# Feature products spread over four steps, x tiles requested before the last query store, prologue and exponentials reordered, x1 reloaded in small parts

## The chip, the cores and the metric

The kernel runs on one core of a Trainium2 chip. TensorE multiplies, VectorE, ScalarE and GpSimd (POOL) do the elementwise work, SyncE issues nearly all DMAs. The metric is device time in microseconds of one execution. The engines run their own instruction streams in order and meet at semaphores.

## The reference

Two layers over N = 4096 rows of D = 512, with a symmetric sparse matrix adj (4096 x 4096):

```python
q, k, v = x @ Wq.T + bq, x @ Wk.T + bk, x @ Wv.T + bv
a = q @ k.T / sqrt(512) + adj + adj
x = layernorm(x + softmax(a) @ v)              # layer 0
feats = einsum('nf,hfd->hnd', x, W)            # layer 1, 8 heads of 64
dense = leaky_relu(e_self + e_neigh) + NEG_INF * (1 - adj)
out = relu(softmax(dense) @ feats + b)
x = layernorm(x + out)
```

With NEG_INF = -1e10 and values of adj up to 5.4, each row of layer 1 picks the neighbour with the largest adj (the kernel proves this on the way, and has a general path that isn't run here). So layer 1 is: compute feats for all rows, find each row's largest entry of adj, gather that row of feats, add, normalise.

## The kernel before

All products are made of two float16 parts (high and low): a product of two such operands is three matmuls. Q and K are folded: scores are (x M + c) x^T with M = Wq^T Wk.

**Prologue.** Eight groups g of 512 rows. TensorE computes for each group four value tiles (48 matmuls, banks S0 and S1 in turn, `split_product` on line 635; the third tile waits until VectorE has emptied the bank, `vf_set`) and then the query product (48 matmuls into O0 to O3). ScalarE makes high parts (`x_hi`, `value_hi`, `query_hi`), VectorE empties the value banks (`value_rows`, L979) and makes low parts (`x_lo`, `value_lo`: L963, `query_lo`: L996). GpSimd adds values crosswise (`value_sums`). Per pair of value tiles the chain is GpSimd, ScalarE, VectorE, and GpSimd's buffer is single. SyncE stores x (`x_scratch`), value sums (`vsum_scratch`) and queries (`y_scratch`) and then loads adj and x tiles for the main loop.

**Main loop.** 16 blocks b of 256 query rows, 16 chunks k of 256 keys; c = 16 b + k. One pass of the loop, a step s, has on TensorE the scores of chunk s (24 matmuls, L607) and the values of chunk e = s - 19 (21 matmuls, L684). Per step come 2 x tiles of 256 KB (`xring`, a ring of NX = 5), adj^T (256 KB), value sums (128 KB, a ring of 3), and about one piece of adj (256 KB) for the search of the largest entry. For chunk e: VectorE adds adj (`add`, L1101), takes maxima (L1113), later subtracts the maximum (`subtract`, L1094), ScalarE takes the exponential (L901), GpSimd sums halves (L556, L557), VectorE differences (L1079), ScalarE copies the high parts (L808, narrow 128x128 and wide 128x768), GpSimd makes the low parts (L567, L570), and TensorE multiplies. In the last block VectorE makes the wide low part instead (`last_lo`, L1087). Buffers `pfc` and `pc` are double.

When block b is through its values, its "turn" comes at step 16(b+1)+19: VectorE combines the banks (`combine`), normalises two row tiles j = 0, 1 (`statistics`, `normalise_x1`, at offsets 1 and 2, and 3 and 4 from the turn), and TensorE transposes x1 (8 matmuls, L724) at offset 3 + 2j and multiplies it by W1 (`feats`, 12 matmuls of 512 columns, L735) at offset 4 + 2j, all into bank X. The four W1 tiles of a row tile (`xring<-w_scratch`, 256 KB each) go through the same ring as x. VectorE empties X (`evict_feats`, L1179), and the next tile's transposes wait for that (`f_set`). `block_at(s, offset)` gives the block that stands at that offset; SyncE waits in the same order (`x1_set`, `f_set`) to store x1 and feats. The order of loads is the list `stream`.

**End.** x1 is reloaded in four parts of 2 MB (the last 1.5 MB) during the last block (`load_x1`). After the last block's feats are stored, GpSimd issues 32 indirect loads of feats rows (L589), VectorE and ScalarE add and normalise eight groups, and SyncE stores them.

## Time and profile before

| | us |
|---|---|
| median of 3 runs | 1775.04 |
| lowest, highest | 1771.71, 2446.5 |
| profiled execution, its own time | 1778.22 |
| its span, first to last instruction | 1776.3 |
| TensorE busy | 1600.0 (90%) |
| VectorE busy | 1352.9 (76%) |
| GpSimd busy | 1245.2 (70%) |
| ScalarE busy | 621.6 (35%) |

The chain of work that ended last is 64% TensorE, 11% VectorE, 8% GpSimd, 7% DMA. In the views, PE is TensorE's matmuls, PEld its weight loads, DVE VectorE, ACT ScalarE, POOL GpSimd, SPq SyncE's queue; L607 is line 607 of the kernel; "out<-in" names the tiles; a bracket gives the idle time ahead of an instruction and what ended it. A matmul row's length overlaps the next by about 0.16 us, so steps are read from start to start. The clock column is the share of 2.4 GHz that TensorE was granted.

### The profile page before, as it was taken

The page shows a single profiled execution, that of the slowest core. Times are in us where ns is not written, and L with a number is a line of the kernel's source. Part 1 is how long each engine was busy: PE and PEld are TensorE (multiplying, and loading weights), DVE is VectorE, ACT ScalarE, POOL GpSimd, SP SyncE. Part 2 cuts the span into 40 slices and gives each one's busy share as a digit, 9 for nine tenths or more (in the row PEclk, how much of TensorE's full clock was granted, in tenths as well). Part 3 has the DMA queues.
Part 4 walks back from the last instruction along what each step waited for, and adds up shares of the span by engine and source line. Part 5 has one row for each costly group of instructions (what it writes and reads, how often), then busy time and mean ns, then how long its engine had stood idle before and what let it go on. Part 6 is the DMA issues. An engine that isn't in the chain of part 4 may idle for free.

```text
span 1776.3 us, 36165 instructions
## 1 busy us (share of the span) xinstructions
PE 1600.0 (90%) x13172; PEld 1283.5 (72%) x13172; DVE 1352.9 (76%) x2241; ACT 621.6 (35%) x1085; POOL 1245.2 (70%) x1461
## 2 busy tenths in 40 slices
PE   7798979999999999999999999999999999997820
PEld 3333468888888888888887878788888787875600
DVE  5544437887988888888797888788888888877646
ACT  4343402333333333333332333333333333333427
POOL 3323304988887888788887888888888888886533
PEclk9899989999999999999999999999999999998955
DMA  6434278888888888888888888888888888881668
GB/s 240 151 112 146 107 243 290 265 263 271 260 282 259 287 255 294 263 290 255 280 257 265 262 282 262 276 260 282 263 291 259 284 258 276 252 266 57 200 209 292
DMA packets 281859, 438.13 MB, mean 247 GB/s; under 512 B 26960, under 2 KB 127312, under 8 KB 281680
## 3 DMA queue, kind: packets, MB, share of 16 engines
q1 hardware_dynamic: 276560, 419.01, 73.3%
q0 software_dynamic: 5120, 16.78, 2.9%
q8 instruction: 106, 1.74, 0.4%
q14 instruction: 73, 0.60, 0.1%
HBM read 390.60 MB, written 45.09 MB: 245 GB/s over the span
## 4 chain that ended last, share of the span: by engine, by line
PE 64%; DVE 11%; POOL 8%; DMA 7%; issue 5%; ACT 4%; SPq 1%; ACTq 0%; DVEq 0%; POOLq 0%
PE S L607 32%; PE O L684 26%; DMA xring<-w_scratch 5%; PE X L735 3%; DVE big L963 2%; POOL big L589 1%; POOL pfc L556 1%; POOL pc L570 1%; DMA vsum<-vsum_scratch 1%; PE X L724 1%; DVE pfc L1079 1%; POOL pfc L557 1%; POOL pfc L525 1%; DVE cand L1052 1%; DVE big L1101 1%
## 5 line engine op out<-in xcount | busy, mean ns | idle before, releaser
L607 PE MATMUL S<-yb,xring 128*128 128x256 f16 x6144 | 710.2, 273 | 11.4 <-DMA xring<-x_scratch 11.4
L607 PEld LDWEIGHTS S<-yb,xring 128*128 128x128 f16 x6144 | 602.5, 98 | 84.9 <-issue 11.9
L684 PE MATMUL O<-big,pc 128*128 128x256 f16 (+1 forms) x4608 | 599.8, 276 | 11.8 <-DMA vsum<-vsum_scratch 5.8
L808 ACT ACTIVATE pc<-pfc 128x128 f16<-128x128 f32 (+1 forms) x512 | 289.1, 574 | 862.1 <-PE O L684 549.0
L684 PEld LDWEIGHTS O<-big,pc 128*128 128x128 f16 x4608 | 453.2, 99 | 80.8 <-issue 7.8
L570 POOL TENSOR_TENSOR pc<-pfc,pc 128x768 f16<-128x768 f32 x240 | 396.0, 1650 | 137.1 <-ACT pc L808 136.1
L1101 DVE TENSOR_TENSOR big<-S,big 128x512 f32<-128x512 f32 x256 | 175.6, 686 | 177.5 <-PE S L607 177.0
L556 POOL TENSOR_TENSOR pfc<-pfc 128x256 f32<-128x256 f32 x256 | 233.1, 911 | 79.8 <-ACT pfc L901 79.1
L1113 DVE TENSOR_TENSOR mx<-mx,big 128x512 f32<-128x512 f32 x240 | 238.6, 994 | 8.2
L565 POOL TENSOR_TENSOR sacc<-sacc,pfc 128x256 f32<-128x256 f32 x240 | 212.6, 886 | 0.0
L1079 DVE TENSOR_TENSOR pfc<-pfc 128x256 f32<-128x256 f32 x256 | 186.4, 728 | 0.1
L901 ACT ACTIVATE pfc<-big 128x512 f32<-128x512 f32 x256 | 157.2, 614 | 60.2 <-DVE big L1094 60.1
L1094 DVE TENSOR_TENSOR big<-BC,big 128x512 f32<-128x512 f32 x256 | 173.8, 679 | 2.2 <-PE BC L713 1.4
L1052 DVE MAX8 cand<-piece 128x8 f32<-128x512 f32 x256 | 172.4, 679 | 1.8 <-DMA piece<-in_adj 1.8
L567 POOL TENSOR_TENSOR pc<-pfc,pc 128x128 f16<-128x128 f32 x256 | 116.2, 454 | 79.3 <-ACT pc L808 78.9
L557 POOL TENSOR_TENSOR pfc<-pfc 128x128 f32<-128x128 f32 x256 | 152.5, 596 | 0.0
L684 PE MATMUL O<-vsum,pc 128*128 128x256 f16 x768 | 127.4, 275 | 0.0
L523 POOL TENSOR_TENSOR pfc<-big 128x512 f32<-128x512 f32 x16 | 20.2, 1266 | 151.5 <-DVE big L979 104.9
L735 PE MATMUL X<-xring,x1T 128*128 128x512 f16 x384 | 96.5, 394 | 23.0 <-DMA xring<-w_scratch 20.4
L735 PEld LDWEIGHTS X<-xring,x1T 128*128 128x128 f16 x384 | 36.2, 100 | 71.0 <-DMA xring<-w_scratch 33.4
L684 PEld LDWEIGHTS O<-vsum,pc 128*128 128x128 f16 x768 | 75.8, 99 | 9.3
L607 PE MATMUL S<-big,xring 128*128 128x512 f16 x192 | 49.5, 421 | 15.4 <-DVE big L979 15.1
(130 smaller groups left out, 1190.8 us busy)
## 6 DMA issues: line engine op xcount, KB each, us to landing
xring<-x_scratch SPq DMA_DIRECT2D x512, 256.0 KB, 3.9
big<-in_adjT SPq DMA_DIRECT2D x256, 256.0 KB, 4.2
piece<-in_adj SPq DMA_DIRECT2D x256, 256.0 KB, 3.9
vsum<-vsum_scratch SPq DMA_DIRECT2D x256, 128.0 KB, 3.3
xring<-w_scratch SPq DMA_DIRECT2D x128, 256.0 KB, 3.9
big<-in_xT SPq DMA_DIRECT2D x8, 1024.0 KB, 8.3
yb<-y_scratch SPq DMA_DIRECT2D x16, 512.0 KB, 4.8
hc<-in_x SPq DMA_DIRECT2D x32, 256.0 KB, 4.7
```

The costliest lines, as they stand in the source:

```text
L556: pool.tensor_tensor(buf[:, 512:768], buf[:, 0:256], buf[:, 256:512], ALU.add).then_inc(sums_set, 1)
L565: pool.tensor_tensor(total, total, buf[:, 512:768], ALU.add).then_inc(sum_done, 1)
L570: pool.tensor_tensor(parts[:, 1, P:7 * P], buf[:, 3 * P:9 * P], parts[:, 0, P:7 * P], ALU.subtract).then_inc(lo_rest, 1)
L607: mm = pe.matmul(psum, sta(a, k), mov(b, k), start=(k + a + b == 0), stop=(k == n - 1 and a == 1))
L684: mm = pe.matmul(dst, pc[:, e % 2, a, sta * P:(sta + 1) * P], mov, start=start, stop=(k == NP - 1 and a == 1 and closes))
L735: mm = pe.matmul(X[:, :], x1T[:, a, kc, :], weights[:, m, :], start=(kc + a + m == 0), stop=(kc == KC - 1 and a == 1))
L808: return nc.scalar.activation(dst, src, ACT.Copy, scale=scale)
L1052: dve.max(cand[:, q, :], piece[:, p % NSC, :]).then_inc(cand_set, 1)
L1079: dve.tensor_tensor(buf[:, 768:1024].rearrange("p (k n) -> p k n", k=2), quarters[:, :, 1, :], quarters[:, :, 0, :], ALU.subtract).then_in ...
L1094: dve.tensor_tensor(slot, BC[:, :].rearrange("p (o n) -> p o n", o=1).broadcast_to([P, 2, QB]), slot, ALU.subtract).then_inc(sub_done, 1)
L1101: dve.tensor_tensor(slot, S[c % 2][:, :], slot, ALU.add).then_inc(add_done, 1)
L1113: dve.tensor_tensor(mx[:, :], mx[:, :], slot, ALU.max).then_inc(max_done, 1)
```

## The change

1. A row tile's feature product is spread: its four parts kc go into four successive steps, offsets 4 to 7 for j = 0 and 9 to 12 for j = 1; transposes at offsets 3 and 8, evictions at 7 and 12. The last block keeps all four in one step, at offsets 4 and 6, but uses banks S0 and X for the transposes and O0 and O1 for the products, and evicts at 7 and 8. LAST grows by 6 steps.
2. SyncE issues the first 3 adj and 5 x tiles at the start of the last prologue group. TensorE's wait for all value sums (`v_lo`) moves from the scores to the first values.
3. In the prologue VectorE makes x's low part of the next group behind the first two value rows, and both ScalarE and VectorE handle two query parts ahead of the second value pair.
4. In the main loop ScalarE takes the exponential of chunk e+1 ahead of the copies of chunk e.
5. x1 is reloaded in 15 parts of 512 KB, one a step, from chunk 242 on.

The diff, cut (`load_passing` and `load_adj` moved up unchanged):

```diff
-        LAST = turn(NB - 1) + 8
+        LAST = turn(NB - 1) + 14
...
 
+
+        def transposes_at(s, j):
+            b = block_at(s, 3 + 5 * j)
+            last = block_at(s, 3 + 2 * j)
+            return last if last == NB - 1 else b if b is not None and b < NB - 1 else None
+
+        def feats_at(s, j):
+            parts = [(block_at(s, 4 + 5 * j + kc), kc) for kc in range(KC)]
+            last = block_at(s, 4 + 2 * j)
+            if last == NB - 1:
+                return [(last, kc) for kc in range(KC)]
+            return [(b, kc) for b, kc in parts if b is not None and b < NB - 1]
+
+        def evict_at(s, j):
+            b = block_at(s, 7 + 5 * j)
+            last = block_at(s, 7 + j)
+            return last if last == NB - 1 else b if b is not None and b < NB - 1 else None
+
+        def x1_bank(t):
+            return S[0][:, :] if t == NT - JB else X[:, :]
+
+        def feats_bank(t):
+            return X[:, :] if t < NT - JB else O[t % JB][:, :]
+
+
         def passing():
             for s in range(LAST):
                 for c in scores_at(s):
                     yield s, ("x", c, 0)
                     yield s, ("x", c, 1)
                 for j in range(JB):
-                    b = block_at(s, 4 + 2 * j)
-                    if b is not None:
-                        for kc in range(KC):
-                            yield s, ("w", b * JB + j, kc)
+                    for b, kc in feats_at(s, j):
+                        yield s, ("w", b * JB + j, kc)
 
         stream = list(passing())
...
+                if g == NG - 1:
+
+                    for c in range(AHEAD):
+                        load_adj(c)
+                    for k in range(2):
+                        sp.wait_ge(x_out[k], 16 * (NG // 2))
+                    sp.wait_ge(yp_ready, (NG - 1) * KC)
+                    for i in range(NX):
+                        load_passing(i)
                 if g + 2 < NG:
                     load_x(g + 2)
...
-            def load_x1(e):
-                first, last = 2 * e * EG, min(2 * (e + 1) * EG, NT - JB)
+            def load_x1(b):
+                first, last = b * JB, (b + 1) * JB
                 for j in range(JB):
-                    sp.wait_ge(x1_out[j], 16 * (last // JB))
+                    sp.wait_ge(x1_out[j], 16 * (b + 1))
 
...
                 sp.dma_start(x1r[:, first:last, :],
-                             x1_d[first * P:last * P, :].rearrange("(j p) n -> p j n", p=P)).then_inc(x1r_in[e], 16)
-
-            for c in range(AHEAD):
-                load_adj(c)
-            for k in range(2):
-                sp.wait_ge(x_out[k], 16 * (NG // 2))
-            sp.wait_ge(yp_ready, (NG - 1) * KC)
-            for i in range(NX):
-                load_passing(i)
+                             x1_d[first * P:last * P, :].rearrange("(j p) n -> p j n", p=P)).then_inc(x1r_in[b // 4], 16)
+
...
-                    b = block_at(s, 4 + 2 * j)
+                    b = evict_at(s, j)
...
-                e, r = divmod(s - (NC - NP + 6 + LAG), 5)
-                if r == 0 and 0 <= e < NE // 2:
-                    load_x1(e)
+                if 0 <= s - (NC - NP + 2 + LAG) < NB - 1:
+                    load_x1(s - (NC - NP + 2 + LAG))
...
+                if e == 0:
+                    pe.wait_ge(v_lo, NP)
                 pe.wait_ge(vs_in[e % NVS], (e // NVS + 1) * 16)
...
                 if t % JB == 0:
                     pe.wait_ge(rinv_set, t // JB + 1)
-                else:
+                elif t < NT - JB:
                     pe.wait_ge(f_set, t)
+                dst = x1_bank(t).bitcast(F16)
                 for a in range(2):
                     for kc in range(KC):
-                        mm = pe.transpose(X16[:, (a * KC + kc) * P:(a * KC + kc + 1) * P], x1h[:, a, kc * P:(kc + 1) * P],
+                        mm = pe.transpose(dst[:, (a * KC + kc) * P:(a * KC + kc + 1) * P], x1h[:, a, kc * P:(kc + 1) * P],
                                           ident16[:, :])
                 mm.then_inc(x1T_done, 1)
 
-            def feats(t):
-                pe.wait_ge(x1T_set, t + 1)
-                for kc in range(KC):
-                    i = place["w", t, kc]
-                    weights = xring[:, i % NX, :].rearrange("p (a n) -> p a n", a=2)
-                    pe.wait_ge(x_in[i % NX], (i // NX + 1) * 16)
-                    for a, m in ((0, 0), (0, 1), (1, 0)):
-                        mm = pe.matmul(X[:, :], x1T[:, a, kc, :], weights[:, m, :], start=(kc + a + m == 0),
-                                       stop=(kc == KC - 1 and a == 1))
-                    mm.then_inc(f_part, 1)
+            def feats(t, kc):
+                if kc == 0:
+                    pe.wait_ge(x1T_set, t + 1)
+                    if t >= NT - JB:
+                        pe.wait_ge(c_added, 8 * NB)
+                i = place["w", t, kc]
+                weights = xring[:, i % NX, :].rearrange("p (a n) -> p a n", a=2)
+                pe.wait_ge(x_in[i % NX], (i // NX + 1) * 16)
+                for a, m in ((0, 0), (0, 1), (1, 0)):
+                    mm = pe.matmul(feats_bank(t), x1T[:, a, kc, :], weights[:, m, :], start=(kc + a + m == 0),
+                                   stop=(kc == KC - 1 and a == 1))
+                mm.then_inc(f_part, 1)
 
...
-            pe.wait_ge(v_lo, NP)
             for s in range(LAST):
...
-                    b = block_at(s, 3 + 2 * j)
+                    b = transposes_at(s, j)
                     if b is not None:
                         transpose_x1(b * JB + j)
-                    b = block_at(s, 4 + 2 * j)
-                    if b is not None:
-                        feats(b * JB + j)
+                    for b, kc in feats_at(s, j):
+                        feats(b * JB + j, kc)
...
-                query_hi(g, 0)
+                for jc in range(2):
+                    query_hi(g, jc)
                 value_hi(2 * g + 1)
-                for jc in range(1, KC):
+                for jc in range(2, KC):
                     query_hi(g, jc)
...
@@ -881,6 +908,15 @@
                     scaled(cb[:, 1, 0:DHALF], O[1][:, 0:DHALF], 1.0).then_inc(c_copied, 1)
                     act.wait_ge(o_done, 3 * b + 3)
                     scaled(cb[:, 0, DHALF:D], O[2][:, 0:DHALF], 1.0).then_inc(c_copied, 1)
...
+                e = s - LAG + 2
+                if 0 <= e < NC:
...
+                    nc.scalar.activation(pfc[:, e % 2, 0:512], ring[:, e % SLOTS, :], ACT.Exp, scale=-2.0
+                                         ).then_inc(exp_done, 1)
                 e = s - LAG + 1
                 if 0 <= e < NC:
                     if e >= 2:
...
                     act.wait_ge(sums_set, 2 * e + 2)
                     act.wait_ge(diff_set, e + 1)
                     scaled(pc[:, e % 2, 0, P:7 * P], buf[:, 3 * P:9 * P], 1.0).then_inc(hi_done, 1)
-                e = s - LAG + 2
-                if 0 <= e < NC:
...
-                                         ).then_inc(exp_done, 1)
                 for j in range(JB):
                     b = block_at(s, 2 + 2 * j)
                     if b is not None:
@@ -909,13 +936,14 @@
                             act.wait_ge(x1T_done, t)
                         src = xr[:, j, :] if b < NB - 1 else x1r[:, t, :]
                         scaled(x1h[:, 0, :], src, X1_UP).then_inc(x1_hi, 1)
-                    b = block_at(s, 3 + 2 * j)
+                    b = transposes_at(s, j)
                     if b is not None:
                         t = b * JB + j
                         act.wait_ge(x1T_done, t + 1)
                         if t >= 1:
                             act.wait_ge(f_part, t * KC)
-                        scaled(x1T[:, :, :, :].rearrange("p a c n -> p (a c n)"), X16, 1.0).then_inc(x1T_set, 1)
+                        scaled(x1T[:, :, :, :].rearrange("p a c n -> p (a c n)"), x1_bank(t).bitcast(F16), 1.0
+                               ).then_inc(x1T_set, 1)
...
-                for i in range(GT):
+                for i in range(2):
+                    value_rows(g * GT + i)
+                if 1 <= g < NG - 1:
+                    x_lo(g + 1)
+                for i in range(2, GT):
                     value_rows(g * GT + i)
                 value_lo(2 * g)
-                query_lo(g, 0)
+                for jc in range(2):
+                    query_lo(g, jc)
                 value_lo(2 * g + 1)
-                for jc in range(1, KC):
+                for jc in range(2, KC):
                     query_lo(g, jc)
-                if g + 2 < NG:
-                    x_lo(g + 2)
...
-                dve.scalar_tensor_tensor(out=cb[:, j, :], in0=X[:, :], scalar=1.0 / (W_UP * X1_UP), in1=b1b[:, :],
+                dve.scalar_tensor_tensor(out=cb[:, j, :], in0=feats_bank(t), scalar=1.0 / (W_UP * X1_UP), in1=b1b[:, :],
...
-                    b = block_at(s, 4 + 2 * j)
+                    b = evict_at(s, j)
...
-                    dve.wait_ge(x1r_in[e // 2], 16)
+                    dve.wait_ge(x1r_in[e // 2], 16 * 4 if e < NE - 2 else 16 * 3)
```

What stands in a row on VectorE in the prologue, at the start of group 3 (the groups count from 0). Before (L963 on `hc` or `xring` is x's low part, L979 the value rows, L996 the query parts, L963 on `big` and `vsum` the values' low parts):

```order
L963 SCALAR_TENSOR_TENSOR xring<-big,xring 128x512 x4
L1036 TENSOR_REDUCE u<-big 128x4x8
L979 SCALAR_TENSOR_TENSOR big<-S,big 128x512 x4
L963 SCALAR_TENSOR_TENSOR big<-big 128x512
L963 SCALAR_TENSOR_TENSOR big<-pfc,big 128x1024
L963 SCALAR_TENSOR_TENSOR vsum<-pfc,vsum 128x256
L996 TENSOR_TENSOR yb<-pfc,yb 128x2x256
L963 SCALAR_TENSOR_TENSOR big<-big 128x512
L963 SCALAR_TENSOR_TENSOR big<-pfc,big 128x1024
L963 SCALAR_TENSOR_TENSOR vsum<-pfc,vsum 128x256
L996 TENSOR_TENSOR yb<-pfc,yb 128x2x256 x3
```

After (L991, L1007 and L1024 are the same three):

```order
L1024 TENSOR_TENSOR yb<-pfc,yb 128x2x256 x2
L1067 TENSOR_REDUCE u<-big 128x4x8
L1007 SCALAR_TENSOR_TENSOR big<-S,big 128x512 x2
L991 SCALAR_TENSOR_TENSOR xring<-big,xring 128x512 x4
L1007 SCALAR_TENSOR_TENSOR big<-S,big 128x512 x2
L991 SCALAR_TENSOR_TENSOR big<-big 128x512
L991 SCALAR_TENSOR_TENSOR big<-pfc,big 128x1024
L991 SCALAR_TENSOR_TENSOR vsum<-pfc,vsum 128x256
L1024 TENSOR_TENSOR yb<-pfc,yb 128x2x256 x2
L991 SCALAR_TENSOR_TENSOR big<-big 128x512
L991 SCALAR_TENSOR_TENSOR big<-pfc,big 128x1024
L991 SCALAR_TENSOR_TENSOR vsum<-pfc,vsum 128x256
```

x's low part has moved from the end of the group into the middle of the value rows, and two query parts stand ahead of the second three value parts. The reduce (L1036, then L1067) stays where it was.

On TensorE, the feature product of a block's first row tile. Before (L607 scores, L724 transposes, L735 feature product, L684 values):

```order
L724 MATMUL X<-ident,x1h 128x128 x8
L684 MATMUL O<-big,pc 128x256 x3
L684 MATMUL O<-vsum,pc 128x256 x3
L684 MATMUL O<-big,pc 128x256 x15
L607 MATMUL S<-yb,xring 128x256 x24
L735 MATMUL X<-xring,x1T 128x512 x12
```

After (L750 transposes, L630 scores, L763 feature product, L709 values):

```order
L750 MATMUL X<-ident,x1h 128x128 x8
L709 MATMUL O<-big,pc 128x256 x3
L709 MATMUL O<-vsum,pc 128x256 x3
L709 MATMUL O<-big,pc 128x256 x15
L630 MATMUL S<-yb,xring 128x256 x24
L763 MATMUL X<-xring,x1T 128x512 x3
L709 MATMUL O<-big,pc 128x256 x3
L709 MATMUL O<-vsum,pc 128x256 x3
L709 MATMUL O<-big,pc 128x256 x15
L630 MATMUL S<-yb,xring 128x256 x24
L763 MATMUL X<-xring,x1T 128x512 x3
```

Twelve matmuls in a row have become three in each of four steps, of which two are shown.

On ScalarE, around a block's turn. Before (L808 with `hc` are the combine's copies, with `pc` the high parts, L901 the exponential):

```order
L808 ACTIVATE hc<-O 128x2x256
L808 ACTIVATE hc<-O 128x256 x2
L808 ACTIVATE pc<-pfc 128x128
L808 ACTIVATE pc<-pfc 128x768
L901 ACTIVATE pfc<-big 128x512
L808 ACTIVATE pc<-pfc 128x128
```

After (L918 is the exponential):

```order
L834 ACTIVATE hc<-O 128x2x256
L834 ACTIVATE hc<-O 128x256 x2
L918 ACTIVATE pfc<-big 128x512
L834 ACTIVATE pc<-pfc 128x128
L834 ACTIVATE pc<-pfc 128x768
L918 ACTIVATE pfc<-big 128x512
```

The exponential has moved from behind the two copies to in front of them.

## Rows read from the trace of the kernel before

**Rows 1.** Busy time by stage: window, its length, busy time (instructions), clock, DMA share, GB/s
```profile
42.70:203.80 161.10, 137.12 (x578) 58.81 (x577) 83.74 (x115) 64.22 (x92) 49.73 (x42) 0.89 0.37 128
203.80:224.50 20.70, 20.70 (x97) 9.28 (x95) 9.65 (x15) 8.41 (x15) 6.79 (x6) 1.00 0.30 114
...
370.10:1532.70 1162.60, 1131.23 (x10013) 970.59 (x10012) 976.79 (x1591) 396.64 (x716) 956.36 (x1122) 1.00 0.85 270
```

**Rows 2.** Prologue in time, TensorE: start us, length, instruction [idle before <- releaser]
```profile
110.61 7.86 PE L607 MATMUL S<-big,hc 128*128 128x512 f16 x24 [4.21 <-DVE big L979]
...
138.49 1.89 PE L607 MATMUL S<-big,xring 128*128 128x512 f16 x4 [4.48 <-DVE big L979]
```

**Rows 3.** The same view, VectorE in the same two groups
```profile
105.27 2.50 DVE L963 SCALAR_TENSOR_TENSOR xring<-big,xring 128x512 f16<-128x512 f32 x4 [1.11 <-ACT xring L808]
...
128.66 0.42 DVE L963 SCALAR_TENSOR_TENSOR vsum<-pfc,vsum 128x256 f16<-128x256 f32 x1
```

**Rows 4.** Instructions in time, TensorE, where the scores start
```profile
236.07 4.21 PE L607 MATMUL S<-yb,xring 128*128 128x256 f16 x19 [11.42 <-DMA xring<-x_scratch]
```

**Rows 5.** DMA issues: tile, queue, count, KB each, us to landing
```profile
xring<-w_scratch SPq DMA_DIRECT2D x128, 256.0 KB, 3.9
...
big<-x_scratch SPq DMA_DIRECT2D x3, 2048.0 KB, 8.3
```

**Rows 6.** Instructions in time, TensorE: the row sums that close a block
```profile
370.14 0.50 PE L696 MATMUL X<-vup,sacc 128*128 128x1 f32 x4
...
1532.69 0.51 PE L696 MATMUL X<-vup,sacc 128*128 128x1 f32 x4
```

**Rows 7.** The same view: a wait for weights, and two steps in a row
```profile
948.39 1.33 PE L735 MATMUL X<-xring,x1T 128*128 128x512 f16 x3 [2.16 <-DMA xring<-w_scratch]
...
1241.00 2.78 PE L607 MATMUL S<-yb,xring 128*128 128x256 f16 x24
...
1245.91 2.78 PE L607 MATMUL S<-yb,xring 128*128 128x256 f16 x24
```

**Rows 8.** Who waited for whom, main loop: us in total, times, longest
```profile
PE X L735 <- DMA xring<-w_scratch: 18.7, 17, 2.4
...
PE X L724 <- DVE hc L1179: 10.1, 9, 1.6
...
PEld X L724 <- DVE x1h L963: 4.5, 8, 1.2
```

**Rows 9.** Instructions in time, all engines, at a block's turn
```profile
1182.01 0.41 DVE L1079 TENSOR_TENSOR pfc<-pfc 128x256 f32<-128x256 f32 x1
1182.35 0.68 DVE L1094 TENSOR_TENSOR big<-BC,big 128x512 f32<-128x512 f32 x1
1182.52 0.84 ACT L808 ACTIVATE pc<-pfc 128x768 f16<-128x768 f32 x1 [3.54 <-DVE pfc L1079]
...
1189.08 1.63 POOL L570 TENSOR_TENSOR pc<-pfc,pc 128x768 f16<-128x768 f32 x1
...
1191.23 0.49 PE L684 MATMUL O<-big,pc 128*128 128x256 f16 x3
```

**Rows 10.** Instructions in time, last block: VectorE, ScalarE and TensorE
```profile
1658.21 0.97 DVE L1087 TENSOR_TENSOR pc<-pfc,pc 128x768 f16<-128x768 f32 x1 [0.62 <-ACT pc L808]
...
1661.15 0.61 ACT L901 ACTIVATE pfc<-big 128x512 f32<-128x512 f32 x1
1661.27 0.98 DVE L1087 TENSOR_TENSOR pc<-pfc,pc 128x768 f16<-128x768 f32 x1 [0.62 <-ACT pc L808]
...
1661.85 0.31 ACT L808 ACTIVATE pc<-pfc 128x128 f16<-128x128 f32 x1
...
1666.28 0.82 PE L684 MATMUL O<-big,pc 128*128 128x256 f16 x3 [4.50 <-DMA vsum<-vsum_scratch]
...
1667.53 4.05 PE L684 MATMUL O<-big,pc 128*128 128x256 f16 x18
...
1701.02 0.61 PE L724 MATMUL X<-ident,x1h 128*128 128x128 f16 x8 [0.87 <-DVE hc L1179]
```

56 lines of the change are left out of this document (27 added, 29 removed).

## The prediction

> **What bounds the kernel now.** I read the busy time by stage first, then the order of instructions inside one period of each stage, and the table of waits last. The program has four stages. In the prologue (42.7 to 203.8 us for six of eight groups) TensorE is busy 137 of 161 us at a granted clock of 0.89, and one group without waits takes 20.7 us at full clock [rows 1]. The main loop (370.1 to 1532.7 us) is TensorE's: busy 1131 of 1163 us, clock 1.00, while the DMA engines are 85% busy [rows 1]. Then comes the last query block, in which only values are multiplied, and an end in which indirect loads, VectorE and ScalarE work and TensorE doesn't.
>
> **Prologue.** TensorE waits 4.21 us in the middle of a group's value rows for VectorE, and a group later 4.48 us again; from one such restart to the next it is 27.88 us [rows 2]. The 24 matmuls behind the wait take 7.86 us. What VectorE does while TensorE stands is the low half of x (2.50 us, started only at 105.27) and then a reduce, and only then the value rows that free the PSUM bank [rows 3]. The change puts this x work behind the first two value rows, so that it lies beside the two value tiles that TensorE has by then (20.7/8 = 2.6 us each). It also lets the second query copy go ahead of the second value pair on both engines. The serial chain of value sums (GpSimd, ScalarE, VectorE, twice a group) is not shortened, but in the group that restarts at 110.61 its second round was over at 129.1, 18.5 us later [rows 3], and so fits in 20.7 us. I work the six groups as 6 x 20.7 = 124. Added to that: group 1 keeps a split of W1 behind x's high half, in all about 8 us of ScalarE and VectorE work behind the group's end where TensorE can cover 5.2, hence 3.2 us, perhaps with a slow restart of 1.5 us; groups 2 and 3 keep the reduce, 0.3 us each. Sum 129.5 against 161.1: **31 us gained**, bounds 22 (four of six waits go) and 36 (all, full clock).
>
> *A rule weighed here.* The wait costs more than its length: matmuls ran at half speed for a while, granted clock 0.89 over the stage. The Trainium skill ("TensorE: Matmul & The Clock Gate", Part 1) says that the clock is low by default and that only sustained activity releases it; by that, removing short waits returns more than the waits, which the trace bears out (7.86 us for 24 matmuls that take 20.7/4 = 5.2). The same rule speaks against the change at the end, below.
>
> **Start of the scores.** The prologue's last matmul ends at 224.5 [rows 1], the first scores start at 236.07, after a wait of 11.42 us for x tiles [rows 4], whose requests stand behind the last value and query stores in SyncE's queue. They move ahead of these: five tiles are in the ring long before 224.5, and the scores start at once. But VectorE's last query part is only ready some 3 us after TensorE, and the sixth tile still stands behind that store and three value-sum loads (1.3 us): issued about 4.5 us after the prologue's end, landing 3.9 us later at best [rows 5], 8.5 to 9.5 us. Five tiles last 5 x 1.31 = 6.6 us. So a new stall of 2 to 3 us takes the place of 11.6: **9 us gained**, bounds 6 and 11.
>
> **Main loop, feature matmuls.** From the row sums at 370.14 to those at 1532.69 lie 13 blocks [rows 6], 89.4 us each. A clean step (24 score and 21 value matmuls) is 4.91 us (1241.00 to 1245.91) [rows 7]. 16 steps are 78.6; two feature products of 12 matmuls at 0.216 us 5.2; transposes, broadcast, row sums and the wider first matmuls 2.7: 86.5 us. The other 2.9 us are waits. Before, a tile's four weight tiles follow each other in a ring of five. The fourth is requested only when the step's first x tile is used up, 3.2 us before its turn, and takes 3.9 us or more [rows 5]; so the last three matmuls wait, 2.16 us in the row at 948.39, after which they run slow [rows 7]. In total TensorE waits 18.7 us for weights, and its weight loads longer; and 10.1 us because the next tile's transposes want the bank that VectorE has yet to empty [rows 8]. After the change each step of a feature tile has two x tiles and one weight tile, the step is 5.56 us, and a tile is requested five uses ahead: at least 6.9 us. The second tile's transposes come one step (4 us) after the eviction. Both waits go. DMA per time falls in these steps (1.4 MB in 5.56 us, before 2.2 MB in 7.5), the rate of the others. What stays is the wait for x1's low half (4.5 us of the weight loads' waits over the 13 blocks, 0.3 each [rows 8]). Gain 2.6 us a block, bounds 1.5 and 2.9.
>
> **Main loop, exponentials first.** ScalarE now does the exponential of e+1 ahead of the copies of e. That costs the copies the subtraction (0.68), the exponential (0.61) and handoffs: they come about 1.2 us later, and GpSimd's low part behind them. In plain steps its result has 3 us to spare after that. At a block's turn it has less: the subtraction starts at 1182.35, ScalarE's wide copy at 1182.52, and the next but one low part ends at 1189.08 + 1.63 = 1190.7, TensorE wants it at 1191.23 [rows 9]. A shift of 1.1 us makes it late by 0.5 to 0.6 us, once a block; what this delays further on would otherwise wait for x1. Costs 0.55 a block, bounds 0 (the shift is hidden) and 1.6 (each of three steps late). Net 2.05 us on 14 blocks: **29 us gained**. Where the cover is gone: were the low part late in every step, each tenth of a us would cost 24 us over 240 steps.
>
> **Last block.** Here VectorE makes the low part itself. Before, a step is 3.06 us (1658.21 to 1661.27) [rows 10], since ScalarE's copies and exponential and GpSimd's sums form a ring. With the exponential first, VectorE's low part of e waits for its own subtraction, then the exponential 0.61, the copies 0.31 and 0.84, then 0.97 itself, and a difference of 0.41 and a subtraction of 0.68 follow [rows 9, 10]: with what overlaps and the handoffs 3.6 us. Over the steps 240 to 255, with what TensorE's backlog hides, I count the last start of values 8 to 11 us later by this alone. Against it, the x1 reloads in 2 MB parts (8.3 us to landing) [rows 5] held back the small value-sum loads behind them: a wait of 4.50 us, behind which 18 matmuls take 4.05 us [rows 10], and a shorter one 12 us later. Parts of 512 KB, one a step, end that: 7 to 8 us back. Sum **2.5 us lost**, bounds 12 lost and 6 gained. The low clock belongs to the bound: a step of 3.6 us leaves TensorE idle 1.3, and at the speed shown behind the wait of 4.50 a step's 21 value matmuls take 4.05 x 21/18 = 4.7 us, which is more than the step.
>
> *A rule against this part.* The 2 MB parts landed in 8.3 us, 247 GB/s each alone, a 256 KB tile in 3.9 us, 67 GB/s [rows 5]. The Trainium skill ("DMA: Bandwidth & Descriptors", Rules for kernel authors) wants at least 1 MiB per DMA. By it 15 parts, one after another at the small tile's latency, would be 59 us against 33. By the trace that changes nothing here, for the parts are issued over 15 steps (some 50 us) and nobody wants them before the last block is done.
>
> **After it.** The last tile's transposes use another bank and needn't wait 0.87 us for VectorE [rows 10]; the end is as before. 0.9 us gained.
>
> **Sum.** 1778.2 us is the profiled execution's own time (span 1776.3 and 1.9 around it); less 31, 9, 29 and 0.9, plus 2.5: 1710.8. The median of the runs shown is 1775.0, 3.2 below it; on that scale 1707.6. I say 1708.
>
> **Rivals.**
> - *The turns take it back.* The late low parts cost 1.6 us a block and the feature gain is the low bound of 1.5: the main loop then gives nothing, 1708 + 29 = 1737; half of it 1722. For it: GpSimd is busy 956 of 1163 us [rows 1], so it catches up slowly. Against: its slack in plain steps. Chance 0.17, mostly 1722 to 1737.
> - *The prologue gain stays away*, because the value-sum chain and not the x work sets the group: 1708 + 25 = 1733. For it: the chain runs twice for 9 us. Against: the last group, which has no x work, takes 20.7 us with the same chain [rows 1]. Chance 0.08.
> - *Slower.* ScalarE's new order makes GpSimd the bound in every step: its own work is 4.6 us (956.4 over 208 steps [rows 1]) of the 4.91 to 5.6 of a step, and it breaks even with the whole gain when each of the 240 steps takes 0.29 us longer; at 0.5 us it is 1828. It decides from the point at which the low part ends after 7.5 us of its step's start; I work it to end at 4.4. Chance 0.03.
> - *No reload stall and no cost of the order in the last block*, and all waits gone: 1708 - 13 = 1695 or less. Chance 0.1.
>
> **How the numbers follow.** The forecast (1697 to 1722) has 0.62. From 1690 to 1732 lie the forecast, the better case and most of the first rival, about 0.82. A measurement of this kernel can tell about 2%, that is 1739.5 us. Faster 0.89 (all but the tails of the first two rivals and the third), same 0.08, slower 0.03.
>
> **What would show it.** Right: prologue groups of 20.7 us and its end near 194; scores from there without a gap, with one stall of 2 to 3 us before the sixth tile; blocks of 87.4 us without a wait on weights; a PE wait of about 0.5 us for GpSimd's low part two steps into a block; VectorE's low parts 3.6 us apart in the last block and no wait on value sums. Wrong: groups over 23 us, blocks over 89, feature matmuls that wait for weights, or TensorE at the 1.2 GHz level through the last block.

## The result, and the profile after

The changed kernel takes 1747.1 us (median of 4 runs, 1745.7 to 1751.3). The kernel before took 1774.6 us beside it; the ratio is 0.985, 95% interval 0.983 to 0.988. The gain is 27.5 us where 67 were forecast, and the time lies 25 us above the forecast range (1697 to 1722) and 15 above the wider one (1690 to 1732). The profiled execution took 1745.7 us (span 1743.9; before 1776.3). The spans of the two profiled executions differ by 32.4 us, more than the medians, for the one before was 3.6 us above its median and the changed one 1.4 below; the stages below are compared by these.

The changed kernel by windows: the prologue's six groups, the start of the scores up to the first row sums, the 13 blocks of the main loop, and the last two blocks. Columns: window, length, busy time of PE, PEld, DVE, ACT and POOL with instruction counts, clock, DMA share, GB/s:

```profile
42.70:193.84 151.14, 145.34 (x672) 65.25 (x671) 110.44 (x128) 72.86 (x105) 67.36 (x48) 1.00 0.47 166
193.84:330.34 136.50, 131.99 (x1180) 116.40 (x1179) 104.04 (x145) 29.14 (x55) 73.37 (x87) 0.99 0.85 273
330.34:1495.17 1164.83, 1134.68 (x10012) 967.49 (x10011) 1049.03 (x1591) 384.95 (x715) 954.33 (x1120) 1.00 0.85 270
1495.17:1654.76 159.59, 131.91 (x1084) 106.27 (x1083) 116.62 (x181) 57.32 (x108) 117.82 (x150) 0.95 0.61 192
```

The prologue's end (first row) and the start of the scores came as forecast. TensorE in time, changed kernel, where the prologue ends; three waits are left in the six groups, the longest of them here at 72.03:

```profile
72.03 5.35 PE L630 MATMUL S<-big,xring 128*128 128x512 f16 x24 [3.48 <-DVE big L1007]
...
193.84 6.71 PE L630 MATMUL S<-yb,xring 128*128 128x256 f16 x60
202.69 7.52 PE L630 MATMUL S<-yb,xring 128*128 128x256 f16 x52 [2.13 <-DMA xring<-x_scratch]
```

193.84 answers to 224.50 in [rows 1], and the scores follow without a gap where they started at 236.07 [rows 4]; the new stall of 2.13 us stands before the sixth x tile. The row sums at 370.14 and 1532.69 [rows 6] now stand at:

```profile
330.34 0.50 PE L721 MATMUL X<-vup,sacc 128*128 128x1 f32 x4
...
1495.17 0.51 PE L721 MATMUL X<-vup,sacc 128*128 128x1 f32 x4
```

So 39.8 us had been won at the first mark and 37.5 at the second: 13 blocks take 89.6 us each, before 89.4, forecast 87.4. From 1495.17 to the last row sums at 1654.76 are 159.6 us, before 151.7 (1532.69 to 1684.35): 7.9 us lost. These are the last two blocks: 84.0 and 75.6 us, before 82.8 and 68.9. From there to the end are 89.2 us, before 92.0: 2.8 us won. -39.8 + 2.3 + 7.9 - 2.8 = -32.4, the difference of the spans.

The waits that answer to [rows 8], changed kernel, 330 to 1495 us:

```profile
PEld O L709 <- issue: 40.9, 48, 1.7
...
PE O L709 <- POOL pc L593: 21.8, 34, 1.3
...
PEld X L750 <- DVE x1h L991: 10.7, 13, 2.2
...
PE X L750 <- DVE x1h L991: 7.2, 8, 1.9
...
PEld X L763 <- DMA xring<-w_scratch: 0.5, 2, 0.3
```

The waits for weights (18.7 us) and for the emptied bank (10.1) have gone, as forecast. In their place TensorE waits 21.8 us for GpSimd's wide low part (its weight loads stand still for 40.9 us ahead of the values, in part the same time), and longer for x1's low part (7.2 us against 2.0 before). The 34 waits for GpSimd's low part fall into two kinds. Two steps into each of the 13 blocks there is one of 0.20 to 0.74 us, 0.52 in the mean, in six blocks with a short one of 0.17 or 0.26 in the step behind it. The rest, 13.8 us or 1.06 a block, stand later, among the feature steps, and are 0.38 to 1.26 us long.

### The profile page after: what moved, and what is told of

Read it like the earlier page. It is cut to its first block, busy times and chain, and to the rows that moved or that the text cites. A ratio compares the mean times of both kernels' runs of the same rounds, so it can differ in the third digit from the quotient of the medians.

```text
span 1743.9 us, 36188 instructions
## 1 busy us (share of the span) xinstructions
PE 1590.0 (91%) x13172; PEld 1276.3 (73%) x13172; DVE 1452.9 (83%) x2241; ACT 607.6 (35%) x1085; POOL 1257.9 (72%) x1461
## 3 DMA queue, kind: packets, MB, share of 16 engines
q8 instruction: 106, 1.74, 0.4%
## 4 chain that ended last, share of the span: by engine, by line
PE 54%; DVE 18%; POOL 11%; issue 11%; ACT 5%; DMA 2%; SPq 1%; DVEq 0%; ACTq 0%; POOLq 0%
PE S L630 27%; PE O L709 19%; POOL pc L593 4%; PE O L630 3%; DVE pfc L1110 3%; DVE big L1125 3%; PE X L763 3%; DVE big L1132 2%; ACT pc L834 2%; ACT x1h L834 1%; POOL pfc L579 1%; POOL big L612 1%; DVE cand L1083 1%; DVE mx L1144 1%; DVE big L991 1%
## 5 line engine op out<-in xcount | busy, mean ns | idle before, releaser
L630 PE MATMUL S<-yb,xring 128*128 128x256 f16 x6144 | 709.2, 273 | 2.1 <-DMA xring<-x_scratch 2.1
L630 PEld LDWEIGHTS S<-yb,xring 128*128 128x128 f16 x6144 | 602.1, 98 | 74.8 <-DMA xring<-x_scratch 2.4
L709 PE MATMUL O<-big,pc 128*128 128x256 f16 (+1 forms) x4608 | 600.2, 275 | 42.1 <-POOL pc L593 25.9
L709 PEld LDWEIGHTS O<-big,pc 128*128 128x128 f16 x4608 | 448.3, 99 | 141.6 <-issue 65.9
L918 ACT ACTIVATE pfc<-big 128x512 f32<-128x512 f32 x256 | 161.3, 630 | 949.8 <-DVE big L1125 945.7
L593 POOL TENSOR_TENSOR pc<-pfc,pc 128x768 f16<-128x768 f32 x240 | 407.6, 1698 | 52.8 <-ACT pc L834 52.7
L1144 DVE TENSOR_TENSOR mx<-mx,big 128x512 f32<-128x512 f32 x240 | 284.5, 1185 | 8.2
L579 POOL TENSOR_TENSOR pfc<-pfc 128x256 f32<-128x256 f32 x256 | 248.9, 972 | 57.0 <-ACT pfc L918 56.3
L834 ACT ACTIVATE pc<-pfc 128x128 f16<-128x128 f32 (+1 forms) x512 | 268.1, 562 | 15.4 <-POOL pfc L580 10.7
L590 POOL TENSOR_TENSOR pc<-pfc,pc 128x128 f16<-128x128 f32 x256 | 110.3, 431 | 194.8 <-ACT pc L834 194.7
L1110 DVE TENSOR_TENSOR pfc<-pfc 128x256 f32<-128x256 f32 x256 | 244.6, 956 | 0.0
L588 POOL TENSOR_TENSOR sacc<-sacc,pfc 128x256 f32<-128x256 f32 x240 | 191.9, 800 | 0.0
L1125 DVE TENSOR_TENSOR big<-BC,big 128x512 f32<-128x512 f32 x256 | 173.5, 678 | 1.7 <-PE BC L738 1.4
L580 POOL TENSOR_TENSOR pfc<-pfc 128x128 f32<-128x128 f32 x256 | 142.2, 555 | 0.0
L709 PE MATMUL O<-vsum,pc 128*128 128x256 f16 x768 | 126.9, 275 | 0.0
L546 POOL TENSOR_TENSOR pfc<-big 128x512 f32<-128x512 f32 x16 | 25.5, 1592 | 109.8 <-DVE big L1007 76.0
L763 PE MATMUL X<-xring,x1T 128*128 128x512 f16 x360 | 98.2, 382 | 0.8 <-ACT x1T L834 0.8
L709 PEld LDWEIGHTS O<-vsum,pc 128*128 128x128 f16 x768 | 75.5, 98 | 9.3
L991 DVE SCALAR_TENSOR_TENSOR x1h<-hc,x1h 128x512 f16<-128x512 f32 x30 | 51.2, 1705 | 32.9 <-ACT x1h L834 32.9
L763 PEld LDWEIGHTS X<-xring,x1T 128*128 128x128 f16 x360 | 33.9, 98 | 21.9 <-ACT x1T L834 4.5
```

The costliest lines, as they stand in the source:

```text
L579: pool.tensor_tensor(buf[:, 512:768], buf[:, 0:256], buf[:, 256:512], ALU.add).then_inc(sums_set, 1)
L588: pool.tensor_tensor(total, total, buf[:, 512:768], ALU.add).then_inc(sum_done, 1)
L593: pool.tensor_tensor(parts[:, 1, P:7 * P], buf[:, 3 * P:9 * P], parts[:, 0, P:7 * P], ALU.subtract).then_inc(lo_rest, 1)
L630: mm = pe.matmul(psum, sta(a, k), mov(b, k), start=(k + a + b == 0), stop=(k == n - 1 and a == 1))
L709: mm = pe.matmul(dst, pc[:, e % 2, a, sta * P:(sta + 1) * P], mov, start=start, stop=(k == NP - 1 and a == 1 and closes))
L763: mm = pe.matmul(feats_bank(t), x1T[:, a, kc, :], weights[:, m, :], start=(kc + a + m == 0), stop=(kc == KC - 1 and a == 1))
```

## Experiments

Each ratio is the time over that of the kernel before, measured beside it, with its 95% interval; "run 1" is experiment 1. The edits are shortened to the order of the calls. The numbers of lines are those of each kernel; in the changed kernel L709 are the values, L763 the features, L593 GpSimd's wide low part, L1110 VectorE's differences, L1125 its subtraction, L1118 its low part in the last block, L918 the exponential. "Blocks" means the mean of the first 13 from row sums to row sums, and "the last block" the time from its predecessor's row sums to its own. The kernels of experiments 7, 10 and 11 ran on a chip where the kernel before takes 1783.8 us, and their end is some 10 us longer than in the others; there I compare the stages.

**1. The order of ScalarE undone.**

```diff
+ scaled(pc narrow, e), scaled(pc wide, e)
  activation(Exp, e + 1)
- scaled(pc narrow, e), scaled(pc wide, e)
```

> The changed kernel with one part undone: in every step ScalarE copies the high parts of e first and takes the exponential of e+1 behind them, as before the change. Theory A (the new order of ScalarE eats the feature gain, through GpSimd's low part that comes too late for TensorE: 21.8 us of waits in 13 blocks, and through the overlap of VectorE's and GpSimd's work): blocks go from 89.6 to 86.8 to 87.4 us, 2.2 to 2.8 each, 14 blocks 31 to 39 us, the last block gives 8 to 10 us back, so 1700 to 1710 us. Theory B (the spread feature product itself makes the low parts late, the order is neutral in the main loop): blocks stay at 89 to 89.6, only the last block gains, 1736 to 1745 us.

1692.9 us, ratio 0.954 (0.952 to 0.956). The row sums that open and close its 13 blocks:

```profile
330.07 0.50 PE L721 MATMUL X<-vup,sacc 128*128 128x1 f32 x4
...
1462.03 0.50 PE L721 MATMUL X<-vup,sacc 128*128 128x1 f32 x4
```

Blocks 87.07 us; the last block is 61.5 us, in the changed kernel 75.6; the block before it 80.4 against 84.0. TensorE's waits for GpSimd's low part fall from 21.8 us to 1.0. Theory A holds, and the gain is larger than its 1700 to 1710 us, because the last block gives 14.1 us back where 8 to 10 were expected. The order costs 13 x 2.53 + 3.6 + 14.1 = 50.6 us, and the spans differ by 51.2. This version is the fastest of all that ran.

**2. The order alone, on the kernel before.** The same edit the other way.

> The kernel before with one part of the change alone: ScalarE's exponential of e+1 ahead of the copies of e. Theory A: blocks from 89.4 to 91.5 to 92.2 us (2.2 to 2.8 more), 31 to 39 us over 14 blocks, and the last block 8 to 10 us longer: 1812 to 1825 us. Theory B: blocks stay within 0.3 us of 89.4, with the last block 1778 to 1788 us.

1817.0 us, ratio 1.025 (1.022 to 1.028). Blocks 91.42 us, 2.0 more, a little under the 2.2 to 2.8 of theory A, which holds. By medians the order costs 42 us with the old features and 54 with the new ones (1747.1 less 1692.9); by the spans of the profiled executions 35 and 51. The last block takes 75.5 us here, 6.6 more than in the kernel before.

**3. The old order in the last block only.** `if e < NC - NP` chooses the new order.

> The changed kernel, with ScalarE's old order (copies, then exponential) in the last block's 16 steps alone, the new order in the main loop. If the last block's 7.9 us over the block before come from the order: VectorE's low parts go back from 4.07 to about 3.06 us apart, the last block takes 149 to 152 us from row sums to row sums in place of 159.6, and the time is 1736 to 1740 us. If they come from the reloads of x1 in small parts or from the features of block 14, spread into the last block: 1745 to 1748 us, and the steps stay near 4.07 us. The main loop stays at 89.6 us a block either way.

1733.3 us, ratio 0.977 (0.975 to 0.979): 13.8 us less than the changed kernel and somewhat better than expected. VectorE's low parts are 3.1 us apart again, the last block 61.6 us, blocks 89.7. The whole loss of the last block is the order's.

**4. The front of the change alone, on the kernel before.**

> The kernel before with only the front of the change: x's low part behind the first two value rows, two query parts ahead of the second value pair, and the first x tiles requested before the last query store. Both theories: first row sums at 330 us in place of 370 (39.8 us), main loop at 89.4 a block and the last block as before, so 1735 us, 1733 to 1738. A rival: the early start is partly given back when the loop catches up with its loads, 1742 us or more.

1735.2 us, ratio 0.978 (0.975 to 0.980). First row sums at 330.23, blocks 89.47: nothing is given back. With run 1, in which only the rest of the change is added, the spread features are worth 89.47 - 87.07 = 2.4 us a block.

**5. Where in a block the order costs.** Old order at offsets 0 to 6 from each turn, new order in the other nine steps:

```diff
+ new_order = e >= NC - NP or (s - LAG) % NP > 6
```

> The changed kernel, with ScalarE's old order (copies, then exponential) in the seven steps from each turn on (offsets 0 to 6) of the main loop, and the new order in the nine other steps of a block and in the whole last block. Theory A1 (the new order costs where VectorE's subtraction stands behind the turn's work, since the copies now wait for it; plain steps have the slack): blocks at 87.0 to 87.4 us as in the version with the order undone, 1747 less 13 to 14 times 2.5: 1711 to 1716 us. Theory A2 (the cost lies in all steps, since every low part of GpSimd now overlaps more of VectorE's work): the nine steps keep 9/16 of it, blocks at 88.5 us, 1728 to 1734 us. The last block stays at 75 us either way.

1715.6 us, ratio 0.967 (0.965 to 0.968). Blocks 87.28, last block 75.6. Theory A1: in nine steps of sixteen the order costs 0.2 us a block in all, the rest falls in the seven that begin with the turn, where VectorE also makes x1. VectorE's differences still take 0.89 us in the mean here, against 0.95 in the changed kernel and 0.72 in run 1: outside those seven steps a long difference costs next to nothing.

**6. VectorE's subtraction first.**

```diff
+ subtract(e + 1)
  exp_differences(e)
- subtract(e + 1)
```

> The changed kernel, with VectorE's subtraction of e+1 ahead of its differences of e in every step, so that the exponential, for which ScalarE's copies now wait, can start 0.4 to 0.9 us earlier. If the queue subtraction, exponential, copies, low part is what costs: VectorE's low parts in the last block come 3.4 to 3.6 us apart in place of 4.07 (16 x 0.5 to 0.6, some 8 us less), and the low parts in the turns half as late (1 us a block less, 14 us): 1722 to 1735 us. Rival: the copies only wait for the differences instead, or the waits come from the operations that overlap and not from the queue: 1743 to 1750 us.

1714.9 us, ratio 0.965 (0.963 to 0.967): better than expected. Blocks 87.78, the last block 68.9 us, its low parts 3.46 us apart (from start to start: 1602.05, 1605.53, 1608.99). TensorE's waits for GpSimd's low part fall from 21.8 us to 6.2. The differences' mean fell too, from 0.95 to 0.62 us, while x1's low part stayed long (1.70 us, in the changed kernel 1.76). So this run alone doesn't separate the queue from the overlap.

**7. The overlap.** GpSimd's wide low part is replaced by two fills, which have no inputs; the kernel leaves out the low part of the exponentials:

```diff
- pool.tensor_tensor(low, exp, high, subtract)
+ pool.memset(low, 0); pool.memset(low, 0)
```

> The changed kernel, in which GpSimd's wide low part (128x768, 1.69 us in the mean) is replaced by two fills of the same tile with zeros, one after the other, which read nothing; 256 columns filled take 0.31 us in the prologue, so the two should take 1.6 to 1.9 us. It leaves out the low part of the exponentials, so the probabilities are of lower precision. The new order stays. Theory C (the low part and VectorE's operations with two SBUF inputs hold each other up: the differences take 1.85 us beside it and 0.41 alone, and the subtraction, exponential and copies queue behind them): the mean of the differences falls from 0.96 to 0.6 us or less, that of x1's low part from 1.76 to 1.2, the late low parts go, blocks 87.1 to 88 us, 1715 to 1728 us. Theory D (the queue behind the subtraction is enough by itself, the overlap only goes with it): the differences stay above 0.85 us, or fall while blocks stay within 0.5 us of 89.6, 1740 to 1750 us.

1713.2 us on the slower chip, ratio 0.961 (0.959 to 0.963). Blocks take 86.27 us under the new order, less than the 87.1 to 88 expected. Of TensorE's waits in the 13 blocks one is left:

```profile
PEld X L764 <- DMA xring<-w_scratch: 0.3, 1, 0.3
```

The rows behind that, groups by line and form in the main loop, first the kernel before (mean ns behind the comma):

```profile
L1079 DVE TENSOR_TENSOR pfc<-pfc 128x256 f32<-128x256 f32 x208 | 148.6, 714 | 0.0
...
L1094 DVE TENSOR_TENSOR big<-BC,big 128x512 f32<-128x512 f32 x208 | 141.2, 679 | 1.6 <-PE BC L713 0.9
...
L963 DVE SCALAR_TENSOR_TENSOR x1h<-hc,x1h 128x512 f16<-128x512 f32 x26 | 31.9, 1228 | 22.0 <-ACT x1h L808 22.0
```

the changed kernel:

```profile
L593 POOL TENSOR_TENSOR pc<-pfc,pc 128x768 f16<-128x768 f32 x208 | 351.5, 1690 | 46.2 <-ACT pc L834 46.2
...
L1110 DVE TENSOR_TENSOR pfc<-pfc 128x256 f32<-128x256 f32 x208 | 197.9, 952 | 0.0
...
L1125 DVE TENSOR_TENSOR big<-BC,big 128x512 f32<-128x512 f32 x208 | 140.9, 677 | 0.3
...
L991 DVE SCALAR_TENSOR_TENSOR x1h<-hc,x1h 128x512 f16<-128x512 f32 x26 | 45.8, 1763 | 28.6 <-ACT x1h L834 28.6
```

and the kernel of this run, where L593 and L595 are the two fills:

```profile
L595 POOL MEMSET pc<- 128x768 f16 x208 | 154.6, 743 | 12.0
...
L593 POOL MEMSET pc<- 128x768 f16 x208 | 153.4, 737 | 39.5 <-ACT pc L835 39.5
...
L1126 DVE TENSOR_TENSOR big<-BC,big 128x512 f32<-128x512 f32 x208 | 141.2, 679 | 0.3
...
L1111 DVE TENSOR_TENSOR pfc<-pfc 128x256 f32<-128x256 f32 x208 | 130.3, 627 | 0.0
...
L992 DVE SCALAR_TENSOR_TENSOR x1h<-hc,x1h 128x512 f16<-128x512 f32 x26 | 19.1, 733 | 32.6 <-ACT x1h L835 32.6
```

The differences fall from 952 to 627 ns, x1's low part from 1763 to 733; the subtraction, one of whose inputs is in PSUM, takes 677 to 679 in all three. The two fills start 0.80 us apart and take 1.54 together, 0.15 less than the low part; that is not where a wait of 0.96 us went. Theory C holds. The run takes the overlap away from the differences and from x1's low part at once, so it doesn't say how much each of them cost. The last block, where VectorE makes the low part itself, stays slow (77.1 us).

**8. Big reloads again, on the version of run 1.**

> The changed kernel with ScalarE's old order everywhere (the version with the order undone, 1692.9 us), and x1 reloaded in four parts of 2 MB again, one every five steps. If the small parts are worth what the wait for value sums cost: the wait is back (4 to 6 us for value sums in the last block, with matmuls at half speed behind it), the last block takes 68 to 70 us from its row sums to the last ones in place of 61.5, and the time is 1699 to 1701 us. Rival: the reload was not what the last block waited for and its 61.5 us come from the other banks and the spread of block 14's features: 1692 to 1694 us.

1700.5 us, ratio 0.958 (0.956 to 0.960): inside the expected 1699 to 1701 us, but half of it by luck. The last block takes 64.4 us and not 68 to 70; it loses 2.9 us against the 61.5 of run 1, with waits of 4.0 us for value sums. The other 3.1 us are lost behind it, where I had not looked. Here is the end with big parts (SPq rows are issues; L435 reloads x1, L484 stores feats, L613 is the first indirect load):

```profile
1622.73 0.38 SPq L435 DMA_DIRECT2D big<-x_scratch  x1
...
1626.80 0.69 DVE L1211 SCALAR_TENSOR_TENSOR hc<-O,b1b 128x512 f32<-128x512 f32 x1 [3.64 <-PE O L764]
1633.40 1.04 POOL L613 DMA_INDIRECT big<-feats_scratch,pick  x1 [15.69 <-DMA feats_scratch<-hc]
```

and with small ones:

```profile
1624.58 0.69 DVE L1210 SCALAR_TENSOR_TENSOR hc<-O,b1b 128x512 f32<-128x512 f32 x1 [3.63 <-PE O L763]
1628.04 1.04 POOL L612 DMA_INDIRECT big<-feats_scratch,pick  x1 [13.54 <-DMA feats_scratch<-hc]
```

From the last eviction to the first indirect load are 6.6 us in the one and 3.5 in the other: the last big part is issued just ahead of the two 256 KB stores of feats that everything waits for. The first of them lands 8.8 us after its issue and the second, the last that the indirect loads wait for, after 5.1; with small parts they take 2.9 and 2.0. The 3.1 us are the difference of the second.

**9. x's low part late in the prologue, on the version of run 1.**

> The version with ScalarE's old order (1692.9 us), with x's low part of the group after next at the end of a group on VectorE again, as before the change; the order of the query parts stays new. If x's low part was what TensorE waited for in the middle of the value rows: the prologue's waits are back in the middle groups (4 us and slow matmuls behind them), its end moves from 193.8 to 210 to 222 us, and the time is 1709 to 1721 us. Rival: the order of the query parts alone brings most of the 31 us: 1693 to 1700 us.

1709.1 us, ratio 0.962 (0.960 to 0.964), as expected. First row sums at 348.33, 18.3 us later; the waits in the middle of the groups are back (3.3 to 4.5 us in three of them, with 24 matmuls in 7.0 to 8.1 us behind them).

**10. The old order of the query parts.**

> The version with ScalarE's old order (1692.9 us), with one query part ahead of the second value pair on ScalarE and VectorE and three behind it again, as before the change; x's low part stays behind the first two value rows. x's low part at the end of the group cost 16.2 us of the 31. If the two moves add, this one costs the other 13 to 15 us: 1706 to 1708 us. If either alone already frees TensorE in most groups: 1693 to 1699 us.

1713.5 us, ratio 0.960 (0.958 to 0.962) on the slower chip; first row sums at 338.77, 8.7 us later and not 13 to 15. With run 9 these are 27 of the 31 us: each move brings a share, and neither alone frees TensorE.

**11. The x tiles requested late.**

> The version with ScalarE's old order (1692.9 us), with the first adj and x tiles requested behind the last value and query stores again, and TensorE's wait for all value sums in front of the scores. The prologue keeps its new order. Forecast for this part was 9 us (6 to 11): the prologue ends at 193.8, the scores start 11 to 12 us later, no stall before the sixth tile: 1699 to 1704 us. Rival: the late start is made good by queues that stand fuller, 1693 to 1696 us.

1714.4 us, ratio 0.961 (0.958 to 0.963) on the slower chip; first row sums at 341.09, 11.0 us later. TensorE waits 10.39 us for x tiles. About 3 of the 11 us lie ahead of it, in a prologue in which one group ran slow (24 matmuls in 7.04 us, in run 1 5.35); without them the part is worth about 8 us, where 9 were forecast.

## Why the prediction was wrong, step by step

By the spans 67.4 us were forecast and 32.4 came, 35.0 less. The first 13 blocks miss 29.0 of them (26.7 won were forecast, 2.3 were lost), and 25.7 of these are the price of the exponentials' order. The last two blocks miss 7.4 (0.5 lost forecast, 7.9 measured), the front 0.2; the end was 1.9 better (rounding makes up the rest).

**Prologue, 31 us: right.** 30.7 us (224.5 to 193.8). Three waits of 3.5, 0.6 and 1.7 us stayed, 5.8 in all, where I had added 5.3 to six clean groups; that these agree so well is partly luck, for 1.5 of mine were a slow restart that didn't come, and the third wait is longer than I thought. Both moves carried it: x's low part 18 us (run 9), the query parts 9 (run 10).

**Start of the scores, 9 us: right.** 39.8 - 30.7 = 9.1, with a stall of 2.13 us before the sixth tile.

**Feature matmuls, 2.6 us a block: right.** 2.4 by runs 1 and 4; both waits went. A block without any wait takes 86.27 us (run 7), 86.5 was worked out.

**Exponentials first, 0.55 us a block: this step failed.** It is 2.5, beyond the upper bound of 1.6. That bound was three steps, each late by 0.5, from the durations of the old schedule. The wait that I had worked out came as forecast: at the turn TensorE waits 0.52 us a block for GpSimd's low part. What failed is the path behind it: I took what is delayed later in the block to be covered by the wait for x1, and put the overlap of GpSimd's and VectorE's work at nothing. There the order costs another 1.06 us a block in waits for GpSimd's low part, and more for x1's. Here is the third feature step of a block in the changed kernel, all engines but the weight loads:

```profile
1256.43 1.97 DVE L991 SCALAR_TENSOR_TENSOR x1h<-hc,x1h 128x512 f16<-128x512 f32 x1 [1.15 <-ACT x1h L834]
...
1258.32 0.68 DVE L1132 TENSOR_TENSOR big<-S,big 128x512 f32<-128x512 f32 x1
...
1259.87 0.94 DVE L1110 TENSOR_TENSOR pfc<-pfc 128x256 f32<-128x256 f32 x1
...
1260.73 0.68 DVE L1125 TENSOR_TENSOR big<-BC,big 128x512 f32<-128x512 f32 x1
...
1261.44 0.63 ACT L918 ACTIVATE pfc<-big 128x512 f32<-128x512 f32 x1 [5.05 <-DVE big L1125]
...
1261.98 1.03 ACT L834 ACTIVATE pc<-pfc 128x128 f16<-128x128 f32 x2
...
1263.09 1.74 POOL L593 TENSOR_TENSOR pc<-pfc,pc 128x768 f16<-128x768 f32 x1 [0.30 <-ACT pc L834]
...
1263.25 1.85 DVE L1110 TENSOR_TENSOR pfc<-pfc 128x256 f32<-128x256 f32 x1
...
1264.97 0.49 PE L709 MATMUL O<-big,pc 128*128 128x256 f16 x3 [0.96 <-POOL pc L593]
1265.03 0.68 DVE L1125 TENSOR_TENSOR big<-BC,big 128x512 f32<-128x512 f32 x1
...
1265.74 0.63 ACT L918 ACTIVATE pfc<-big 128x512 f32<-128x512 f32 x1 [2.73 <-DVE big L1125]
```

x1's low part meets GpSimd's and takes 1.97 us. The add and the rest of VectorE's queue shift, the subtraction comes at 1260.73, the exponential has waited 5.05 us for it, and only then the copies run; GpSimd's low part starts at 1263.09 and TensorE has waited 0.96 us when it comes. And the ring closes (each of these operations now waits for another one of them): the differences, started 0.16 us behind that low part, take 1.85 us in place of 0.41 and delay the next subtraction to 1265.03. I had put the delay at the subtraction, exponential and handoffs, 1.2 us, and I had looked for the step with the least slack at the turn. There this block waits 0.29 us (at 1236.36). The larger wait is five steps on, at 1264.97, and in eight of the 13 blocks there is one more at the transposes, for x1's low part. Before, the copies of e needed nothing but the sums and differences of e; the subtraction of e+1 could be late without holding them up. The edit took that slack away and put work that two engines hold up for each other into one chain. Loosening either link helps: the subtraction ahead of the differences gives 1.8 us a block back (run 6), a low part that doesn't hold VectorE up 3.3 (run 7), and then TensorE waits for nothing but 0.3 us of weights.

I had no term for that overlap. The Trainium skill ("SBUF — State Buffer", section on SBUF's two separate sides) has the rule: VectorE and GpSimd share a port pair as an exclusive lock, and a VectorE operation with two SBUF inputs blocks against a GpSimd one that reads SBUF. By it a difference that starts 0.16 us behind a low part of 1.74 waits some 1.6 us and then takes its 0.41, an estimate of 2.0. The trace has 1.85, and the subtraction with an input in PSUM is not touched: it agrees to 0.15 us.

**Last block, 2.5 us lost: wrong, 6.7** (75.6 against 68.9), and the block before it loses 1.2 more where 2.05 were to be won. VectorE's low parts were put 3.6 us apart and stand 4.06 apart, where nothing else comes between. VectorE and ScalarE in the changed kernel:

```profile
1636.68 1.23 DVE L1118 TENSOR_TENSOR pc<-pfc,pc 128x768 f16<-128x768 f32 x1 [1.63 <-ACT pc L834]
...
1637.06 1.17 POOL L580 TENSOR_TENSOR pfc<-pfc 128x128 f32<-128x128 f32 x1
1637.84 0.67 DVE L1110 TENSOR_TENSOR pfc<-pfc 128x256 f32<-128x256 f32 x1
...
1638.44 0.68 DVE L1125 TENSOR_TENSOR big<-BC,big 128x512 f32<-128x512 f32 x1
...
1639.15 0.63 ACT L918 ACTIVATE pfc<-big 128x512 f32<-128x512 f32 x1 [2.50 <-DVE big L1125]
1639.68 1.03 ACT L834 ACTIVATE pc<-pfc 128x128 f16<-128x128 f32 x2
...
1640.74 1.24 DVE L1118 TENSOR_TENSOR pc<-pfc,pc 128x768 f16<-128x768 f32 x1 [1.63 <-ACT pc L834]
```

The ring is the one that I named, but beside GpSimd's sums (L580) the low part takes 1.23 us and not 0.97, and the differences 0.67 and not 0.41; those 0.5 us a step are the miss. The order costs 14.1 us in this block and 3.6 in the one before, 8 to 11 were forecast. The reloads gave back 2.9 us in it and not 7 to 8. The rest of what run 1 gained there over the kernel before (61.5 against 68.9 us, less 2.9, so 4.5) was not in the forecast and made up for part of the miss; I haven't split it between the banks and the features of block 14. The sum had a second fault: it took one effect from the other as if they were independent. Under the new order the last block takes 75.5 us without any other part of the change (run 2) and 75.6 with all of them; VectorE's ring hides whatever they give.

In these steps TensorE was at its upper level of 2.4 GHz, 15 value matmuls in 1.80 us, as in the main loop. Earlier in the block it was not: behind waits of 7.11 us (at 1602.39, for x1's low part) and of 3.11 the same 15 matmuls take 2.56 and 3.41 us, and the granted clock is 0.76 from 1600 to 1620. The second of them:

```profile
1617.09 0.80 PE L709 MATMUL O<-big,pc 128*128 128x256 f16 x3 [3.11 <-DVE pc L1118]
...
1618.32 3.41 PE L709 MATMUL O<-big,pc 128*128 128x256 f16 x15
```

**Behind it, 0.9 us: 2.8, by another cause.** Run 8 shows that it is the last reload, no longer in the way of the feats' stores, and not the bank: with the new banks and big reloads the end takes 91.9 us, before 92.0.

**The rivals.** "The turns take it back" (chance 0.17) came true for the main loop: the order costs 2.5 us a block where the rival had 1.6, the features give 2.4 where it had 1.5, and the loop gives nothing. Its 1737 us were passed mostly because the last two blocks lost 7.4 us more than forecast. "No cost of the order in the last block" (1695 us or less) did not come; 1692.9 is what run 1 took without the order anywhere. The prologue's rival and "slower" fell.

**The rule on 1 MiB per DMA**, weighed in the prediction, would have had the small parts slower. They were better by 6 us (2.9 + 3.1, run 8), not for their own sake: nobody waits for them, but small urgent transfers no longer wait behind large ones.

## What to carry to other kernels

When an operation is moved ahead of others in an in-order queue, list what the ones behind it now wait for, and look for the step in which that is latest, not for the step that is tight today. Durations of VectorE and GpSimd operations hold for one alignment: for every pair that a shift can bring side by side, take the long duration of the row, not the short one, and look whether the pair closes a ring. And undo each part of a bundle by itself: here the other parts brought 83.6 us (1776.3 less 1692.7) and one cost 51.

## What the runs showed of the hardware

- VectorE's 128x256 float32 difference with both inputs in SBUF took 0.41 us alone, 0.94 beside GpSimd's sums and 1.85 beside its 128x768 low part; the 128x512 low part of x1 took 0.69 at the end of the kernel, where GpSimd is idle, and up to 1.98. GpSimd is held up too: its 128x256 sum took 0.71 at the least and 1.18 beside such an operation. With one input in PSUM VectorE's 128x512 subtraction took 0.66 to 0.69 in every step of every kernel.
- A 256 KB store of feats took 2.0 to 4.6 us to land beside reloads of 512 KB (run 1, last block and behind it), and 7.8 to 8.8 us with a reload of 2 or 1.5 MB issued up to 4 us ahead of it (run 8).
- The end with its indirect loads took 88 to 92 us on two chips and 98 to 100 on a third, with the same main loop (87.06 and 87.07 us a block); the cause was not looked for.
